# Second attention of a two-layer block: values of both batches in the same columns, quotients joined by TensorE, a third score buffer

## The reference, cut to what matters

```
Q = query @ W_q.T + b_q;  K = key @ W_k.T + b_k;  V = value @ W_v.T + b_v   # 16 heads of 8 features
scores  = einsum('bhqd,bhkd->bhqk', Q, K) / sqrt(8)
attn    = softmax(scores, axis=-1)
context = einsum('bhqk,bhkd->bhqd', attn, V)
output  = context.reshape(B, Sq, 128) @ W_o.T + b_o      # added to x
```

## Time and profile before

| | us |
|---|---|
| median of 3 runs | 249.6 |
| the three runs | 252.74, 249.60, 249.31 |
| the profiled execution | 252.5 |
| its span, first to last instruction | 250.6 |
| PE busy in the span | 211.7 (84%) |
| DVE busy | 183.2 (73%) |
| ACT busy | 139.9 (56%) |
| POOL busy | 145.7 (58%) |
| mean granted TensorE clock | 0.927 of full speed |

### The profile page before, as it was taken

How to read it: one execution, slowest core, us unless ns; L and a number is a source line. 1 busy time by engine, 2 the same in 40 slices (tenths; PEclk the granted TensorE clock), 3 DMA queues, 4 the chain that set the end, 5 groups by cost and what they waited for, 6 DMA issues and landing times.

```text
span 250.6 us, 5877 instructions
## 1 busy us (share of the span) xinstructions
PE 211.7 (84%) x2010; PEld 144.2 (58%) x2010; DVE 183.2 (73%) x500; ACT 139.9 (56%) x240; POOL 145.7 (58%) x184
## 2 busy tenths in 40 slices
PE   8979999977699999888756579989985989999970
PEld 2425558935255655455545467667764658878750
DVE  7671343877888888876889998689789576766655
ACT  2141115495955544434699867876783565656640
POOL 7637807033199787865899975681486730345530
PEclk9995559998999999979999968999999799999998
DMA  6910441201002110182300020022000125011124
GB/s 218 395 37 3 136 106 55 73 0 31 2 4 61 37 34 29 41 202 86 86 0 3 1 88 0 4 86 84 0 4 0 57 65 132 13 45 37 42 76 126
DMA packets 12890, 15.64 MB, mean 62 GB/s; under 512 B 1744, under 2 KB 9808, under 8 KB 12736
## 3 DMA queue, kind: packets, MB, share of 16 engines
q1 hardware_dynamic: 10736, 12.77, 16.9%
q0 software_dynamic: 736, 1.53, 1.9%
q10 hardware_dynamic: 1392, 1.00, 1.2%
HBM read 11.18 MB, written 3.06 MB: 57 GB/s over the span
## 4 chain that ended last, share of the span: by engine, by line
PE 52%; DVE 17%; ACT 9%; DMA 8%; issue 8%; POOL 4%; SPq 1%; DVEq 0%; ACTq 0%; POOLq 0%
DMA attention_or_experts<-ctx_v 4%; PE ps L1456 3%; PE ps L1371 3%; PE ps L1458 3%; PE ps L1309 3%; PE ps L1457 3%; PE ps L1681 3%; POOL slots_x L578 3%; ACT kM L655 2%; PE ps L1384 2%; PE ps L1666 2%; PE ps L1551 2%; PE ps L1473 2%; PE ps L1668 2%; PE ps L1414 2%
## 5 line engine op out<-in xcount | busy, mean ns | idle before, releaser
L778 ACT ACTIVATE ps<-ps 128x512 f32<-128x512 f32 x47 | 27.4, 584 | 26.9 <-PE ps L1600 17.1
L1219 DVE SCALAR_TENSOR_TENSOR attention_or_experts<-ps,attention_or_experts 128x512 f16<-128x512 f32 x47 | 31.7, 683 | 7.7 <-ACT attention_or_experts L783 7.5
L583 POOL DMA_INDIRECT slots_y<-kM,kS x15 | 14.4, 958 | 23.7 <-DVE kM L1242 22.6
L783 ACT ACTIVATE attention_or_experts<-ps 128x512 f16<-128x512 f32 x47 | 27.7, 593 | 0.0
L1616 PE MATMUL ps<-keys_or_scores,attention_or_experts 128*128 128x128 f16 x128 | 23.9, 224 | 3.7 <-issue 2.6
L1309 PE MATMUL ps<-idle 128*128 128x512 f16 x82 | 22.3, 425 | 3.8 <-ACT kT L614 1.6
L1617 PE MATMUL ps<-keys_or_scores,attention_or_experts 128*128 128x128 f16 x128 | 23.9, 224 | 0.0
L1618 PE MATMUL ps<-keys_or_scores,attention_or_experts 128*128 128x128 f16 x128 | 23.9, 223 | 0.0
L408 POOL TENSOR_TENSOR rstd<-ve,minus_half 128x4 f32<-128x4 f32 x8 | 8.3, 1039 | 23.1 <-DVE ve L832 23.1
L677 ACT ACTIVATE attention_or_experts<-ps 128x512 f32<-128x512 f32 x18 | 10.8, 598 | 19.2 <-PE ps L1458 19.2
L479 POOL TENSOR_TENSOR keys_or_scores<-kT,keys_or_scores 128x512 f16<-128x512 f32 x16 | 18.5, 1158 | 2.4
(11 more groups left out here) (253 smaller groups left out, 692.6 us busy)
## 6 DMA issues: line engine op xcount, KB each, us to landing
raw<-w_second SPq DMA_DIRECT2D x5, 512.0 KB, 3.4
raw<-w_first SPq DMA_DIRECT2D x9, 192.0 KB, 2.8
raw<-w_second SPq DMA_DIRECT2D x6, 256.0 KB, 2.6
attention_or_experts<-ctx_v SPq DMA_DIRECT2D x1, 1056.0 KB, 9.3
slots_x<-kS SPq DMA_DIRECT2D x1, 990.0 KB, 6.9
kS<-slots_x SPq DMA_DIRECT2D x3, 264.0 KB, 3.4
rw<-rows ACTq DMA_DIRECT2D x1, 512.0 KB, 6.7
ctxT<-ctx_t SPq DMA_DIRECT2D x1, 512.0 KB, 6.7
```

The costliest lines, as they stand in the source:

```text
L778: a.activation(up_bank(n), up_bank(n), ACT.Gelu, scale=1 / (XS * XS)).then_inc(s["gelu"], 1)
L783: a.activation(ehi[:, n % 4, :], up_bank(n), ACT.Copy, scale=HS).then_inc(s["hhi1"], 1)
L1219: v.scalar_tensor_tensor(elo[:, n % 4, :], up_bank(n), HS, ehi[:, n % 4, :], ALU.mult, ALU.subtract)\
```

## The change

1. `weighted_values` uses 64 stationary columns instead of 128: one product for each batch, with that batch's 18 columns of values. The products of the lower and upper half alternate, six per pair of heads, 48 per tile instead of 24, with 18 moving columns instead of 36. Both batches' results now lie in the same 144 PSUM columns, on their own partitions.
2. `sums_of_weights` becomes one instruction of 128 partitions instead of two of 64.
3. `divide`, `negative_part` and `numbers_only` are replaced by two instructions `quotients(t, 0)` and `quotients(t, 1)`: max(value, 0) and min(value, 0), each multiplied by the reciprocal, from PSUM to two halves of `o1c` in SBUF. The quotients are no longer written to PSUM.
4. `transpose_values` was one transpose; it becomes two fp32 products with the identity that add the two parts in PSUM.
5. `prob` gets a third buffer: the subtraction of tile t waits for POOL's tile t-3 instead of t-2.
6. Behind the loop, the division of tiles 6 and 7 is done in one go in step 0 and 2, instead of in steps 0 and 1, and 2 and 3. The wait for the transpose of the tile before, which stood at `numbers_only`, stands at the first of the two quotients.

```diff
+        prob_third = sb("prob_third", [P, H1 * S])
...
-        o1n = sb("o1n", [P, H1, D1])
-        o1c = sb("o1c", [P, 2, E])
+        o1c = sb("o1c", [P, 2, 2, E])
...
+        def prob_of(t):
+            return prob_third[:] if t % 3 == 2 else prob[:, t % 3, :]
...
             def subtract_largest(t):
                 v.wait_ge(s["smax"], t + 1)
-                v.wait_ge(s["plo_ready"], reached(t - 1))
-                v.tensor_tensor(prob[:, t % 2, :].rearrange("p (h k) -> p h k", k=S), scores_of(t),
+                v.wait_ge(s["plo_ready"], reached(t - 2))
+                v.tensor_tensor(prob_of(t).rearrange("p (h k) -> p h k", k=S), scores_of(t),
...
+            def values_of(t):
+                return values_bank(t)[:, 0:16 * 9].rearrange("p (h e) -> p h e", e=9)
             def sums_of_weights(t):
                 v.wait_ge(s["av"], t + 1)
-                for q, ov in halves(t):
-                    last = v.tensor_scalar(rs1[q, :].rearrange("p (c d) -> p c d", d=2).unsqueeze(3), ov[:, :, :, 8:9],
-                                           0.5 * PS * VS, None, ALU.max)
-                last.then_inc(s["den1"], 1)
+                v.tensor_scalar(rs1[:].unsqueeze(2), values_of(t)[:, :, 8:9], 0.5 * PS * VS, None, ALU.max).then_inc(s["den1"], 1)
...
-            def divide(t):
+            def quotients(t, sign):
                 v.wait_ge(s["rec1"], t + 1)
-                for q, ov in halves(t):
-                    last = v.tensor_tensor(quotients(t)[q, :].rearrange("p (c d e) -> p c d e", d=2, e=D1), ov[:, :, :, 0:8],
-                                           rs1b[q, :].rearrange("p (c d) -> p c d", d=2).unsqueeze(3)
-                                           .to_broadcast([S, 8, 2, D1]), ALU.mult)
-                last.then_inc(s["mul1"], 1)
-            def negative_part(t):
-                v.wait_ge(s["mul1"], t + 1)
-                v.tensor_scalar(o1n[:].rearrange("p h d -> p (h d)"), quotients(t), 0.0, None, ALU.min).then_inc(s["min1"], 1)
-            def numbers_only(t):
-                v.wait_ge(s["min1"], t + 1)
-                v.wait_ge(s["oTp"], reached(t - 1))
-                v.scalar_tensor_tensor(o1c[:, t % 2, :], quotients(t), 0.0,
-                                       o1n[:].rearrange("p h d -> p (h d)"), ALU.max, ALU.add).then_inc(s["o1_ready"], 1)
+                if sign == 0:
+                    v.wait_ge(s["oTp"], reached(t - 1))
+                last = v.scalar_tensor_tensor(o1c[:, t % 2, sign, :].rearrange("p (h e) -> p h e", e=D1), values_of(t)[:, :, 0:8], 0.0,
+                                              rs1b[:].unsqueeze(2).to_broadcast([P, H1, D1]), (ALU.max, ALU.min)[sign], ALU.mult)
+                if sign == 1:
+                    last.then_inc(s["o1_ready"], 1)
...
                 if i >= 3:
-                    divide(i - 3)
+                    quotients(i - 3, 0)
                 if 4 <= i < NT - 1:
                     x_stats(i - 4)
...
                 if i >= 3:
-                    negative_part(i - 3)
-                if i >= 3:
-                    numbers_only(i - 3)
+                    quotients(i - 3, 1)
...
                 for c in range(8):
-                    o = values_bank(t)[:, c * 36:(c + 1) * 36]
-                    hi, lo = (pT[:, t % 2, part, c * P:(c + 1) * P] for part in range(2))
-                    mm(o, hi, v1hi[:, 2 * t:2 * t + 2, c, :], start=True, stop=False)
-                    mm(o, hi, v1lo[:, 2 * t:2 * t + 2, c, :], start=False, stop=False)
-                    last = mm(o, lo, v1hi[:, 2 * t:2 * t + 2, c, :], start=False, stop=True)
+                    for part, val, first, final in ((0, v1hi, True, False), (0, v1lo, False, False), (1, v1hi, False, True)):
+                        for hf in range(2):
+                            q = slice(hf * S, (hf + 1) * S)
+                            last = mm(values_bank(t)[q, c * 18:(c + 1) * 18], pT[:, t % 2, part, c * P + hf * S:c * P + (hf + 1) * S],
+                                      val[:, 2 * t + hf, c, :], start=first, stop=final)
...
-                pe.transpose(turned(t), o1c[:, t % 2, :], ident).then_inc(s["oTp"], 1)
+                mm(turned(t), o1c[:, t % 2, 0, :], ident, start=True, stop=False)
+                mm(turned(t), o1c[:, t % 2, 1, :], ident, start=False, stop=True).then_inc(s["oTp"], 1)
```

More of the change, by code:

```diff
@@ L245, in build_program @@
             mm1 silu cbp tmul hmul hhi_r hlo_r mm2
-            qproj qhi_ready qS_ready q_moved q_high qS_late bo_added s1 smax ssub phi_ready sexp plo_ready pTp pT_ready av den1 rec1 mul1 min1 o1_ready oTp oT_ready oproj x_att bn3
+            qproj qhi_ready qS_ready q_moved q_high qS_late bo_added s1 smax ssub phi_ready sexp plo_ready pTp pT_ready av den1 rec1 o1_ready oTp oT_ready oproj x_att bn3
             raws1_ready wsp1_hi wsp1_ready mm1b gelu hhi1 hlo1 mm2b gate1_ready yacc
@@ L548, in _ @@
                 pool.wait_ge(s["pTp"], reached(2 * t - 2))
-                pool.tensor_tensor(plo[:, t % 2, :], prob[:, t % 2, :], phi[:, t % 2, :], ALU.subtract).then_inc(s["plo_ready"], 1)
+                pool.tensor_tensor(plo[:, t % 2, :], prob_of(t), phi[:, t % 2, :], ALU.subtract).then_inc(s["plo_ready"], 1)
                 if t < 4:
@@ L726, in exp_scores @@
                 a.wait_ge(s["pTp"], reached(2 * t - 2))
-                a.activation(phi[:, t % 2, :], prob[:, t % 2, :], ACT.Exp, bias=log_ps[:], scale=D1 ** -0.5 / (AS * AS))\
+                a.activation(phi[:, t % 2, :], prob_of(t), ACT.Exp, bias=log_ps[:], scale=D1 ** -0.5 / (AS * AS))\
                     .then_inc(s["phi_ready"], 1)
                 a.wait_ge(s["phi_ready"], t + 1)
-                a.activation(prob[:, t % 2, :], prob[:, t % 2, :], ACT.Exp, bias=log_ps[:], scale=D1 ** -0.5 / (AS * AS))\
+                a.activation(prob_of(t), prob_of(t), ACT.Exp, bias=log_ps[:], scale=D1 ** -0.5 / (AS * AS))\
                     .then_inc(s["sexp"], 1)
@@ L1201, in _ @@
                 if i >= 3:
-                    negative_part(i - 3)
-                if i >= 3:
-                    numbers_only(i - 3)
+                    quotients(i - 3, 1)
             sums_of_weights(5)
             invert_sums(5)
-            divide(5)
-            negative_part(5)
-            numbers_only(5)
+            for sign in range(2):
+                quotients(5, sign)
             low_x(3, 1, 0, 2)
@@ L1254, in _ @@
                     invert_sums(t)
-                    divide(t)
-                if n in (1, 3):
-                    t = 6 + n // 2
-                    negative_part(t)
-                    numbers_only(t)
+                    for sign in range(2):
+                        quotients(t, sign)
                 if n == 3:
```

## The result

| | kernel before | changed kernel |
|---|---|---|
| median of 22 runs each, us | 253.75 | 249.43 |
| lowest and highest, us | 249.31, 259.77 | 247.12, 256.51 |
| ratio, changed to before | | 0.9906 (95%: 0.9877 to 0.9936) |
| profiled execution, its span, us | 252.5, 250.6 | 254.72, 252.9 |

The change makes the kernel 0.9% faster. The interval does not contain 1, so this is more than noise, but it is within 2%. Some executions of either kernel take about 5 us more, those profiled here among them, in whose profiles TensorE runs at half clock (granted 0.50, 1.2 GHz) for 17 us from 19 us on, so the ratio, which compares like with like, is the result, and the two medians are not. Put on the changed kernel's 249.43 the ratio gives 251.8 us for the kernel before.

The account below looks back on a forecast made before the run. TensorE was over half the chain, with VectorE pacing later attention tiles. Loop gains of 2.7 us, less 0.3, 0.1 and 0.1, gave 2.2 less: 249.6 to 247.4 us, range 245.2 to 251.3.

Parts of the forecast that it names:

- the last of the sum: Whole kernel: the 2.2 us saved, taken from the median of 249.6, give 247.4 us.
- VectorE, per tile: VectorE's sums, divisions, minimum and last step: 1.55 us become 0.75, so 0.8 us less per tile where VectorE sets the pace.
- the addition is ready just in time: In the loop: with values products of 0.67 us, VectorE's addition does not wait for TensorE's transposes, which cost nothing there.
- The products: Values products on TensorE: alternate halves overlap, 14 ns per product, 48 in 0.67 us against 0.60 before.
- B: Rival on the values products: 25 ns each, 1.2 us per tile, kernel 0.6 us slower at 250.2; chance 0.28.
- C: Rival: values products' loads and products of one half don't overlap, spacing passes 25 ns, 253.6 or 257.7 us; chance 0.12.
- The joined transposes: TensorE's two fp32 products per tile: 0.44 us, 0.29 more; free in the loop, counted for tiles 4 to 7.
- the ring: Loop chain where TensorE and VectorE wait for each other: last quotient, values, transposes, output product, addition, quotients; no forecast size.
- The loop: Second attention's iterations: 3 gains nothing, 4 gains 0.6 us, 5 and 6 gain 0.8 each, 7 gains 0.5; together 2.7.
- Behind the loop: Between loop and experts: 0.3 us lost to tile 4's transposes ahead of the router, 0.1 to the change of form.
- The experts' first steps: TensorE loses 1.4 us to transposes and values, wins 0.90 of idle time and 0.4 from VectorE: 0.1 lost.
- Rival D's first half: TensorE's clock may stay up after the attention with less idle time ahead; whole rival down to 245.0 us, chance 0.05.

Follow-up runs that it names:

- placement undone: The changed kernel with the second quotient of tiles 6 and 7 back in steps 1 and 3 of the experts; 0.9901 of the kernel before.

## Why the prediction was right or wrong

**The size was right, the base was not.** Forecast were 2.2 us less; 0.9906 of 251.8 is 2.4 less (1.6 to 3.1 by the interval). The forecast time of 247.4 is 2.0 us below the measured 249.43. The step that failed is the last of the sum: "it lies 2.9 above the median, so from the median of 249.6 I forecast 247.4". That median came from three runs, two of which, 249.31 and 249.60, are the lowest of the 22, and none of the 57 runs of this kernel in three later sessions is below 250.53. From 251.8 the same sum gives 249.6. Why those two runs were so short stays open. The steps ahead of the last one add up to the right size, but partly by luck, as follows.

**VectorE, per tile:** 0.8 forecast, 0.76 measured in the iteration of rows 3 (4.57 to 3.81), from two errors that cancel, so by luck. Its own work fell by 1.1, because each of the short instructions adds 0.2 us or less and not 0.25 to 0.29; and "the addition is ready just in time" was wrong by 0.35.

**The products:** the forecast's 14 ns held against B and C, decided by the order of the halves (32 ns in one half, 16 in alternation). 0.67 us per tile was forecast; 0.75 measured. The way there had a wrong reading: 137 less 110 ns was taken for one of the two passes of an fp32 load, but L1404 has 64 load instructions for 32 products, so 137 ns is already one of the two. Those 27 ns for a pair came near the measured 32 by luck. By the rule of the Trainium skill that was weighed, "TensorEngine Tiling (Array Packing)", section "Instruction Overhead", an estimate would have been 1.2 us, which the trace does not bear out. The lower clock does show in this form: in the kernel with the products alone the pairs of tile 4 are 53 to 54 ns apart at a granted clock of 0.50, 1.25 us for the 48, where the old form went only from 25 to 30 ns.

**The joined transposes** were mis-sized, 0.44 against 0.54, and said to cost nothing in the loop. That failed too: they stand in the ring, and without them and the second quotient the wait is gone and the iteration is 0.6 shorter.

**The loop:** iterations 3 to 6 at full clock were 5.42, 5.04, 4.57 and 4.58 in the kernel before and 4.88, 4.55, 3.80 and 3.81 in the changed one (placement undone, whose loop is the same). That is 0.54, 0.49, 0.77 and 0.77; forecast were 0, 0.6, 0.8 and 0.8. Iteration 3 does gain, until the scores of tile 4 come, and the third buffer has about 0.25 of it. Iteration 7, to the last exponential, gained 0.48 in the first two profiles (4.12 to 3.64, the kernel before at the lower clock there); forecast was 0.5.

**Behind the loop:** 0.4 lost was forecast (0.3 and 0.1), and 5.84 to 6.23 is 0.39.

**The experts' first steps:** 0.1 lost was forecast, 0.36 measured (14.76 to 15.12). The transposes there cost 0.39 each more, not 0.29, which is the difference: 0.11 before, 0.50 in TensorE's timeline of the changed kernel, from the first of the two to the experts' product behind them:

```profile
160.69 0.44 PE L1565 MATMUL ps<-pk,o1c 128*128 128x128 f32 x2
160.97 0.39 PE L1566 MATMUL ps<-pk,o1c 128*128 128x128 f32 x2
161.19 0.38 PE L1582 MATMUL ps<-xhi,keys_or_scores 128*128 128x512 f16 x1
```

TensorE's 0.90 us of idle time ahead of tile 7's values did go, but not by the moved quotients: it is gone with the old placement as well.

**Added up at full clock:** the stage is 2.7 us shorter (39.3 to 36.6; 2.3 forecast), and with 0.36 lost in the experts' first steps 2.3 us remain, where 2.2 were forecast. What iteration 3 gained against the forecast pays for what the experts' steps lost against it. As the two first profiles ran, only 1.35 us of the stage shows (39.55 to 38.20). The experts' first product at 156.67 looks like the forecast 156.8, but that is chance: in that profile the first scores already began 1.05 us earlier (118.47 for 119.52), ahead of anything the change touches.

**What no step had:** the collision of norm and POOL, worth 1.8 us where it happens, which the changed kernel escapes with a lead of 0.1 us; and that half clock costs more now. Before, 6.8 us of it in the stage cost 0.3 and 0.9 (39.55 and 40.21 us in the two profiles, against 39.3 with iterations 3 to 6 at full clock). In the changed kernel 3.4 us made iteration 5 longer by 1.58 (5.38 for 3.80), because VectorE then waits 1.93 us for TensorE; where they fell in iteration 3, iterations 3 and 4 together were 0.58 longer (5.93 and 4.08 for 4.88 and 4.55). Rival D's first half came true in that the profiles of the changed kernel have 3.4 us of half clock in the stage in place of 6.8, but at these prices it brought nothing.

## What to carry to other kernels

Products of half width are worth their number only if their order alternates between the halves: 32 ns fell to 16. When an engine that sets the pace is made faster, ask at once which chain ends at its next wait, and add up that chain with its new prices: here it was 0.35 us too long after one short operation had become two. And before taking three runs as the base, look how far they are apart: 249.3 to 252.7 was wider than the 2.2 us that were forecast.

## What was not expected of the hardware

A norm instruction of 0.34 us took 2.14 to 2.24 us when it began beside POOL's subtraction; with 0.04 us of lead it did not, with 0.03 it did (one profile each). TensorE stood still 4.1 to 5.6 us near the experts' middle in all profiles but one, ending about when POOL's eight transfers had landed (in the second profile of the kernel before the transfer that reads them begins at 204.38 us, and VectorE goes on at 204.48); 78 and 156 instructions more on TensorE did not remove or add it, and the cause stays open. The products alone, hidden in the loop, made the kernel 1.3% slower; in its profile most of that stands behind the loop, where products that only keep TensorE busy ran at half clock ahead of needed ones.
